# Expert numbers read into registers once per mixture stage, and the pair loops written out on TensorE and VectorE

## The reference, cut to what matters

```python
logits = xt @ Wr + br                       # xt: layernorm(x), 2048 tokens x 128
probs, idx = top_k(softmax(logits), 2)      # 8 experts, 2 per token
h = layernorm(relu(xt @ W1[e] + b1[e]))     # 128 -> 512, per chosen expert e
y = layernorm(relu(h @ W2[e] + b2[e]))      # 512 -> 128
out = sum of the two experts' y, by gate
x = x + 0.5 * out
```

## Time and profile before

| | us |
|---|---|
| median of 3 runs | 563.18 (562.32 to 565.03) |
| the profiled execution | 562.82 |
| its span in the profile | 560.6 |
| TensorE busy | 455.0 |
| VectorE busy | 372.3 |
| ScalarE busy | 276.2 |
| GpSimd busy | 222.9 |
| TensorE clock granted, mean over the span | 0.905 |

### The profile page before, as it was taken

One profiled execution on the slowest core, in us unless ns is written; L12 is line 12 of the kernel. 1 busy time (PEld: TensorE's weight loads), 2 busy tenths in 40 slices (PEclk: granted clock), 3 DMA queues, 4 the chain that ended last, 5 costly groups with the idle time before them and its releaser, 6 DMA issues.

```text
span 560.6 us, 11828 instructions
## 1 busy us (share of the span) xinstructions
PE 455.0 (81%) x3679; PEld 291.1 (52%) x3683; DVE 372.3 (66%) x1279; ACT 276.2 (49%) x547; POOL 222.9 (40%) x273
## 2 busy tenths in 40 slices
PE   7997988888994358788887987877989999999940
PEld 6653755556662235544545545445636565556630
DVE  4785666665675675787878777667735665666766
ACT  2763555454553137656656567372026554455620
POOL 8705456666543122224134021030055565665430
PEclk9689999998999588888979989896889999999985
DMA  8801111111201400000000000002011111112017
GB/s 247 268 1 39 38 39 37 42 42 39 40 29 52 123 2 1 2 1 2 1 0 0 0 3 1 1 2 76 0 39 33 39 42 37 47 37 42 26 50 203
DMA packets 24020, 24.17 MB, mean 43 GB/s; under 512 B 3817, under 2 KB 18801, under 8 KB 23986
## 3 DMA queue, kind: packets, MB, share of 16 engines
q1 hardware_dynamic: 18690, 12.95, 7.7%
q0 software_dynamic: 5296, 10.78, 6.9%
HBM read 15.43 MB, written 8.26 MB: 42 GB/s over the span
## 4 chain that ended last, share of the span: by engine, by line
PE 40%; DVE 23%; ACT 12%; issue 8%; another core or an unknown queue 7%; DMA 5%; POOL 2%; DVEq 2%; SPq 1%; ACTq 0%; POOLq 0%
PE bank L558 7%; PE bank L576 5%; DVE mx L1211 4%; ACT wide L417 4%; PE bank L1125 3%; PE bank L567 3%; DVE st L757 3%; PE bank L557 2%; DMA yk<-y_scratch 2%; ACT early L910 2%; ACT wide L902 2%; PE bank L1001 2%; PE bank L526 2%; PE bank L1023 1%
## 5 line engine op out<-in xcount | busy, mean ns | idle before, releaser
L304 POOL DMA_INDIRECT xg<-xn_scratch,slot_u x78 | 76.0, 974 | 91.6 <-DVE slot_u L721 45.0
L311 POOL DMA_INDIRECT y_scratch<-yo,dest_u x78 | 77.5, 993 | 73.0 <-ACT yo L432 53.8
L576 PEld LDWEIGHTS bank<-w2c,hT 128*128 128x128 f32 x624 | 76.0, 195 | 37.7 <-issue 37.7
L576 PE MATMUL bank<-w2c,hT 128*128 x624 | 79.2, 281 | 14.2 <-ACT hT L439 13.8
L558 PE MATMUL bank<-w1s,xT 128*128 x156 | 87.8, 645 | 0.0
L439 ACT COPY hT<-bank 128x1024 f32<-128x1024 f32 (+1 forms) x40 | 39.6, 991 | 71.0 <-remote 43.9
L1211 DVE TENSOR_REDUCE mx<-bank 128x4 f32<-128x1024 f32 (+1 forms) x48 | 58.5, 1223 | 20.4 <-PE bank L1032 19.8
L757 DVE BATCH_NORM_STATS2 st<-wide 128x6 f32<-128x512 f32 x78 | 50.3, 685 | 30.1 <-ACT wide L417 19.0
L910 ACT ACTIVATE early<-bank 128x768 f32<-128x768 f32 x64 | 52.0, 815 | 36.1 <-PE bank L1052 35.8
L567 PE MATMUL bank<-ident,wide 128*128 128x128 f32 x312 | 41.3, 275 | 4.7 <-issue 2.2
L772 DVE SCALAR_TENSOR_TENSOR yy<-bank,r,b2p 128x128 f32<-128x128 f32 x78 | 24.6, 351 | 30.7 <-remote 22.5
(11 more groups left out here) (273 smaller groups left out, 857.9 us busy)
## 6 DMA issues: line engine op xcount, KB each, us to landing
yk<-y_scratch SPq DMA_DIRECT2D x32, 128.0 KB, 2.3
w1s<-in_L_ffn_W_dram SPq DMA_DIRECT2D x1, 2048.0 KB, 15.5
xn_scratch<-xn SPq DMA_DIRECT2D x2, 1024.0 KB, 7.0
xg<-xn_scratch,slot_u POOLq DMA_INDIRECT x78
y_scratch<-yo,dest_u POOLq DMA_INDIRECT x78
out_dram<-xs SPq DMA_DIRECT2D x8, 128.0 KB, 2.0
g2b<-in_L_ffn_g_dram POOLq DMA_DIRECT2D x1, 512.0 KB, 5.1
early<-in_L_attn_Wq_dram SPq DMA_DIRECT2D x1, 64.0 KB, 8.7
```

The source lines that it names most:

```text
L304: pool.indirect_dma_start(out=xg[:, u, :], out_offset=None, in_=xn_dram, in_offset=bass.IndirectOffsetOnAxis(ap=slot_u[:, n:n + 1], axis=0 ...
L311: pool.indirect_dma_start(out=y_dram, out_offset=bass.IndirectOffsetOnAxis(ap=dest_u[:, 2 * p + j:2 * p + j + 1], axis=0), in_=yo[:, p % 2 ...
L576: last = pe.matmul(bank[7][:, j * DIM:(j + 1) * DIM], hT[:, u, j, c * P:(c + 1) * P], w2c[:, bass.ds(e * (FC * DIM) + c * DIM, DIM)], star ...
```

## The change

`experts` now reads all five words (tiles 0, 8, 16, 24, 32) in one go and returns the numbers of all 39 tiles. TensorE calls it once per stage, ahead of the first `hidden`; VectorE calls it once, behind the first `stats1`. The hardware loops of both engines are gone: all 20 bodies are written out, with constants in the place of loop registers. The other engines' programs are the same.

```diff
-def experts(eng, eid, n, count):
-
-    v = eng.value_load(eid[0:1, bass.ds(n, 1)], min_val=0, max_val=NE ** PACK - 1)
-    return [(v >> (3 * k)) & (NE - 1) for k in range(count)]
+def experts(eng, eid):
+
+    words = [eng.value_load(eid[0:1, n:n + 1], min_val=0, max_val=NE ** PACK - 1) for n in range(0, SLOT_TILES, PACK)]
+    return [(words[n // PACK] >> (3 * (n % PACK))) & (NE - 1) for n in range(SLOT_TILES)]
...
-            e = experts(pe, eid, 0, 6)
+            e = experts(pe, eid)
             hidden(0, 0, e[0:2])
             pe.wait_ge(s_w2c, 2)
             pe.wait_ge(s_b2c, 2)
             pe.wait_ge(S["gTc"], 1)
-            for n in range(2):
-                body(n, 0, n, e[2 * n:])
-            with pe.Fori(1, PAIRS // 2 - 2) as i:
-                e = experts(pe, eid, i * 4, 6)
-                for u in range(2):
-                    body(i * 2 + u, i, u, e[2 * u:])
             left = [min(2, max(0, SLOT_TILES - 2 * p)) for p in range(PAIRS + 2)]
-            e = experts(pe, eid, 2 * PAIRS - 8, 7)
-            pe.wait_ge(s_be2x, 1)
-            for n in range(PAIRS - 4, PAIRS):
+            for n in range(PAIRS):
+                if n == PAIRS - 4:
+                    pe.wait_ge(s_be2x, 1)
                 if n == PAIRS - 1:
                     shared_bias(0)
-                body(n, n // 2, n % 2, e[2 * (n - PAIRS + 4):], kx=left[n + 2], kh=left[n + 1], k=left[n])
+                body(n, n // 2, n % 2, e[2 * n:], kx=left[n + 2], kh=left[n + 1], k=left[n])
...
             stats1(0, 0)
-            e = experts(dve, eid, 0, 2)
-            body(0, 0)
-            body(1, 1, e)
-            with dve.Fori(1, PAIRS // 2 - 2) as i:
-                e = experts(dve, eid, i * 4 - 2, 4)
-                for u in range(2):
-                    body(i * 2 + u, u, e[2 * u:2 * u + 2])
-            e = experts(dve, eid, 2 * PAIRS - 10, 8)
-            for n in range(PAIRS - 4, PAIRS):
-                body(n, n % 2, e[2 * (n - PAIRS + 4):2 * (n - PAIRS + 4) + 2], kh=left[n + 1])
-            e = experts(dve, eid, SLOT_TILES - 1, 1)
-            y_part(PAIRS - 1, (PAIRS - 1) % 2, e)
-            y_norm(PAIRS - 1, (PAIRS - 1) % 2, e)
+            e = experts(dve, eid)
+            for n in range(PAIRS):
+                body(n, n % 2, e[2 * n - 2:2 * n] if n else None, kh=left[n + 1])
+            y_part(PAIRS - 1, (PAIRS - 1) % 2, e[2 * PAIRS - 2:])
+            y_norm(PAIRS - 1, (PAIRS - 1) % 2, e[2 * PAIRS - 2:])
```

## The result

The changed kernel takes 579.62 us (median of 4 runs, 576.64 to 582.73), the kernel before 564.00 in runs beside it (4 runs, 562.32 to 565.03): a ratio of 1.0297, 95% interval [1.0236, 1.0358]. So it is slower by 3.0%, where 0.7% was forecast: the sign was right, the time lies 7.6 us above the end of the range. The profiled execution took 580.56 us, 17.7 us more than that of before, with a span of 578.4 us.

What follows compares the result with a forecast made beforehand. TensorE was taken as busiest (455.0 of 560.6 us), with late semaphores costing 17.9 us. Forecast: 562.8 + 5.5 (reads) - 1.7 (branches) = 566.6, on the median 567.0 us, 0.7% slower; 8-in-10 range 550 to 572.

Steps and rivals of the forecast that it cites:

- What bounds the kernel: Whole kernel: TensorE busiest, 455.0 of 560.6 us; late TensorE semaphores in the two mixture loops cost 17.9 us.
- Four more reads on TensorE: Ahead of the first `hidden` in each stage: 0.69 us a read, uncovered, 5.5 us more for both stages.
- Branches and reads gone from the loop: TensorE's loop: seven branches and eight reads less, covered in `f1`, showing in `f2`; gain 1.7 us (0 to 3).
- VectorE's reads and back edges: VectorE: four more reads fall in idle time behind the first `stats1`; branch and read less gain nothing; 0.
- More code: Bodies written out need instruction blocks fetched where the loop needed none; taken as 0 (0 to 3 us).
- Held signals: Mixture loops: TensorE semaphores arriving together, late; `hT` waits 12 times; attributed to GpSimd's store and gather chain, unchanged: 0.
- rivals A and B: Held signals in the loops: A, they vanish with the loop, 17.9 us gained, 22%; B, they thin out, half that, 12%.
- Rival D: Mixture stages: `f2` takes up the slower pace of `f1`, 4.2 us more, plus fetch stalls; 572 us, 9% chance.
- Rival C: Ahead of the first `hidden`: the reads overlap, four costing 0.5 us instead of 2.8; 562.5 us, 9% chance.

Runs made afterwards that it cites:

- e7: Kernel before, loops kept, with one more read ahead of TensorE's first `hidden` in each stage: 567.57 us, ratio 1.0092.
- e8: Kernel before, loops kept, with two more reads ahead of TensorE's first `hidden` in each stage: 568.61 us, no ratio given.
- e1: Kernel before, loops kept, with four more reads ahead of TensorE's first `hidden` in each stage: 576.63 us, ratio 1.0235.
- e2: Changed kernel, all bodies written out, but each word read only where its first number is needed: 565.69 us, ratio 1.0035.
- e6: Kernel before with only VectorE as changed, TensorE keeping its loop and reads: 565.21 us, ratio 1.0051.
- e9: Kernel before with filler matmuls between the turned tiles of the first pairs of `f1`: 539.50 us, ratio 0.9936.
- e13: Kernel before, loops kept, with SyncE issuing the stores of `y` as plain DMAs in slot order: 540.26 us, ratio 0.9904.
- e15: Changed kernel with one word read ahead of the first `hidden`, four behind it, and filler matmuls in `f1`: 539.17 us, ratio 0.9926.
- e18: Kernel before, loops kept, with GpSimd issuing the stores of `y` as plain instead of indirect DMAs: 543.90 us, ratio 1.0012.
- e3: Changed kernel with 14 filler matmuls queued on TensorE ahead of the five reads: 567.22 us, ratio 1.0085.
- e12: Kernel before, unchanged, run once for a trace on a chip that showed no held signals: 537.85 us.
- e14: Changed kernel itself, run on a chip without held signals: 556.86 us, ratio 1.0226 against the kernel before.
- e10: Changed kernel with each word read where its first number is needed, plus filler matmuls in `f1`: 538.85 us, ratio 0.9936.
- e16: Kernel before, loops kept, with SyncE issuing the stores of `y` as plain DMAs, on a chip with held signals: 540.58 us, ratio 0.9596.
- e17: Changed kernel with one word read ahead of the first `hidden`, four behind, fillers in `f1`, on a chip with held signals: 560.96 us, ratio 0.9963.

## Why the prediction was right in sign and wrong in size

- **What bounds the kernel.** Right: the loss came from TensorE, and the busy times of the other engines did not move.
- **Four more reads on TensorE, 2.8 us per stage, all on the path.** Right: 2.6 us in `f1`, 3.3 in `f2`, 5.9 together for the 5.5 forecast; e7, e8 and e1 give 0.65 to 0.67 us a read where 0.69 was taken. The 3.3 us of `f2` hold some 0.5 that are not the reads': TensorE had no gap at all there in the profiled execution of before, while eleven other traces with one read in that place (e2, e6, e9 to e13, e15 to e18) have 0.29 to 0.69 us. The floor of some 600 ns that the Trainium skill ("DMA: Bandwidth & Descriptors", latency and other measured facts) gives for a `tensor_load` is no duration that a row here shows (301 ns), but as a price for one further read it is close to these spacings of 650 to 670 ns.
- **The term that was missing: the granted clock.** The prediction had no line for what a pause of 3.3 us does to TensorE's clock. The step that failed is "Nothing covers them … All of it is on the path": it counted the pause by its length alone, and all durations behind it were taken from stretches at full clock. The pause brought 12.2 us more (6.4 up to hT 1, 5.8 up to hT 3), twice the reads. e3 fills the pause and gets the 12.4 us back with the reads still paid; e1 loses the clock with nothing but the reads. The trace of before had the warning and a price. The heads of `f1` and `f2` were at full clock in it, but the page's row of the clock, shown with the result, goes down to 5 and 6 tenths elsewhere, and the very L576 that ends the hole of the earlier trace rows took 3.67 us in place of 2.05 behind 1.51 us of idle time. A pause of 3.3 us could have been given a term from that, and none was made.
- **Branches and reads gone from the loop, -1.7 us.** Too much by half, though within its bounds (0 to 3), and not where it was looked for. Without held signals, where a pure pace can be read, the loop's pairs give 0.16 us for both stages together and hT 17 to hT 20 behind them 0.7 (e12, e14). The 0.24 us of "issue" ahead of L567 was idle time that moved to the next wait, which the prediction named as its lower bound.
- **VectorE's reads and back edges, 0.** Not quite: on a chip that holds signals e6 costs 0.5%, 2.5 us, with two more held signals; on chips without them e10 and e15 lose nothing by it. How VectorE's code comes to bear on the held signals stays open.
- **More code, 0.** Right. The instruction queues moved 28 + 19 packets where it was 20 + 14, and hT 3 to hT 17 shows no stall.
- **Held signals, 0.** Right to within the 2 us of VectorE's part, and with it the weight against rivals A and B: they come 14 times instead of 12 in a program that has no loop on TensorE. The reason given was half right. e16 shows that GpSimd's stores are needed for them. But "at TensorE's best pace GpSimd would be in such a chain almost always" does not mean that this pace can't be had: e12 has exactly this, two pairs in 11.2 us beside the full chain of stores and gathers. The prize was 21.5 us (89.85 + 89.12 less 78.8 + 78.6), above the 17.9 that the prediction worked out from one iteration of each stage, and none of the edits to TensorE's program won any of it.
- **Rival D.** `f2` does take two-pair steps of 13.0 us in places, as it did before in places, and its fourteen pairs took 89.3 us against 89.1: not the 4.2 us. The run landed beyond D for another reason than D's.
- **Rival C.** Out: the gaps grew by the full reads.

## What to carry to other kernels

A further scalar read into a register cost 0.65 us of TensorE's sequencer here; put it where matmuls are queued ahead of it, not ahead of the first matmul that everything else waits for. When an edit opens or lengthens a pause of TensorE at the head of a stage, price it twice: its length, and the stretch behind it at half clock (here 10 to 17 us at 1.2 GHz, about 6 us lost each time in the change); look at the granted clock of the stretch in the trace before taking durations from it. Matmuls that depend on nothing, put into such a wait, gave 0.4 to 0.7% over the kernel before, on chips of both kinds (e9, e10, e15, e17). Writing out the loops gave 0.8 us in the traces of one kind of chip (e12, e14) and cost some 2 us on the other (e6).

## What was not expected of the hardware

- **Signals of TensorE are held on some chips and not on others.** Before took 562.6 to 564.0 us beside the change, e1 to e8, e16 and e17, and 543.2 to 543.8 us beside e9 to e15 and e18, nothing between. The traces of the first group have 11 to 14 remote waits of `hT` (43.0 to 52.6 us), except e16, and those of the second none. The difference, 20 us, is nearly the 21.5 us of hT 3 to hT 17. Whether it is the chip or its state at the time can't be told, since no chip was met in both states.
- **Indirect stores issued by GpSimd take part in it.** Moving them to SyncE as plain DMAs gave 22 us (4.0%) on a chip that holds signals and 0.6 to 1.0% on those that don't. A version that also puts the rows at the tokens' places was not built.
- **The fall of the clock is uneven.** The same program had 13.7 us of half clock at a stage's head in one execution and 17.1 in another (`f1` of the change and e14), and e8, with a gap of 2.07 us, only 3.4. A difference of one or two tenths of a microsecond in the waits ahead of it went with the clock staying up or falling at the head of before's `f1`.
